# The sums of the exponentials on GpSimd: 512 columns at a time into two sums used in turn, in place of 1024 columns into one double sum

## The reference, cut to what matters

```python
q = (query @ wq.T + bq).reshape(B, SQ, H, HD).transpose(0, 2, 1, 3)
k = (key @ wk.T + bk).reshape(B, -1, H, HD).transpose(0, 2, 1, 3)
v = (value @ wv.T + bv).reshape(B, -1, H, HD).transpose(0, 2, 1, 3)
scores = jnp.einsum('bhqd,bhkd->bhqk', q, k) / jnp.sqrt(jnp.asarray(HD, q.dtype))
attn = jax.nn.softmax(scores, axis=-1)
ctx = jnp.einsum('bhqk,bhkd->bhqd', attn, v)
ctx = ctx.transpose(0, 2, 1, 3).reshape(B, SQ, D)
return ctx @ wo.T + bo
```

## Time and profile before

| | |
|---|---|
| time, median of 3 runs | 1692.62 us (1683.69 to 1693.33) |
| time of the profiled execution | 1690.8 us |
| its span, first to last instruction | 1689.0 us |
| PE busy, share of the span | 1619.8 us, 96% |
| DVE busy | 1179.0 us, 70% |
| ACT busy | 950.8 us, 56% |
| POOL busy | 899.7 us, 53% |

### The profile page before, as it was taken

How to read it: one execution, slowest core, us unless ns; L and a number is a source line. 1 busy time by engine, 2 the same in 40 slices (tenths; PEclk the granted TensorE clock), 3 DMA queues, 4 the chain that set the end, 5 groups by cost and what they waited for, 6 DMA issues and landing times. The chain is left out here.

```text
span 1689.0 us, 36984 instructions
## 1 busy us (share of the span) xinstructions
PE 1619.8 (96%) x15589; PEld 1314.5 (78%) x15604; DVE 1179.0 (70%) x1523; ACT 950.8 (56%) x1437; POOL 899.7 (53%) x472
## 2 busy tenths in 40 slices
PE   7999999999999999999999999667998899999999
PEld 6788888888888888888888887556886677777787
DVE  5137888888888888888888887877434577653322
ACT  4347776777767777777777776662103677630000
POOL 0026788888878878888887885002000344522220
PEclk9999999999999999999999999788999799899999
DMA  5332222222222222222222210213422111211001
GB/s 187 75 50 35 36 39 40 39 38 37 38 37 42 36 36 40 41 36 37 37 40 37 40 24 5 80 53 113 165 88 94 38 51 51 65 50 50 28 23 50
DMA packets 310404, 88.75 MB, mean 53 GB/s; under 512 B 259392, under 2 KB 292160, under 8 KB 310240
## 3 DMA queue, kind: packets, MB, share of 16 engines
q1 hardware_dynamic: 310240, 86.39, 22.2%
HBM read 71.67 MB, written 14.68 MB: 51 GB/s over the span
## 5 line engine op out<-in xcount | busy, mean ns | idle before, releaser
L655 POOL TENSOR_TENSOR b_acc<-b_acc,b_s 128x1024 f32<-128x1024 f32 x168 | 563.6, 3355 | 12.4 <-ACT b_s L854 5.3
L892 DVE TENSOR_TENSOR b_s<-b_s,b_mb 128x2048 f32<-128x2048 f32 x128 | 398.0, 3111 | 28.4 <-ACT b_mb L837 28.4
L929 DVE TENSOR_TENSOR b_mx<-b_psS,b_mx 128x512 f32<-128x512 f32 x480 | 330.8, 689 | 93.3 <-PE b_psS L720 80.2
L854 ACT ACTIVATE b_s<-b_s 128x2048 f32<-128x2048 f32 x128 | 244.3, 1909 | 18.3 <-DVE b_s L892 15.2
L871 ACT ACTIVATE b_s<-b_psS 128x2048 f32<-128x2048 f32 x128 | 241.2, 1885 | 20.9 <-DVE b_mx L929 20.9
L43 PE MATMUL b_work<-wvT,cT 128*128 128x512 f32 x496 | 202.9, 409 | 0.0
L43 PE MATMUL b_work<-cT,wkT 128*128 128x512 f32 x496 | 200.3, 404 | 1.7 <-POOL b_ones L636 1.7
L44 PE MATMUL b_work<-wvT,cT 128*128 128x512 f32 x496 | 194.5, 392 | 0.0
L44 PE MATMUL b_work<-cT,wkT 128*128 128x512 f32 x496 | 194.2, 392 | 0.0
L45 PE MATMUL b_work<-wvT,cT 128*128 128x512 f32 x496 | 193.8, 391 | 0.0
L45 PE MATMUL b_work<-cT,wkT 128*128 128x512 f32 x496 | 193.4, 390 | 0.0
(11 more groups left out here) (290 smaller groups left out, 2802.4 us busy)
## 6 DMA issues: line engine op xcount, KB each, us to landing
cin<-in_ctx SPq DMA_DIRECT2D x480, 64.0 KB, 2.4
experts_sb<-in_L_ffn_expert_w SPq DMA_DIRECT2D x8, 1024.0 KB, 5.3
q_scratch<-d_st SPq DMA_DIRECT2D x16, 256.0 KB, 2.3
k_scratch<-d_st SPq DMA_DIRECT2D x16, 256.0 KB, 2.3
e_q<-q_scratch SPq DMA_DIRECT2D x16, 256.0 KB, 2.7
k_sb<-k_scratch SPq DMA_DIRECT2D x16, 256.0 KB, 2.9
cin<-in_ctx SPq DMA_DIRECT2D x4, 512.0 KB, 8.4
b_kT<-in_x SPq DMA_DIRECT2D x4, 512.0 KB, 8.0
```

What stands on the lines that cost most here:

```text
L655: nc.gpsimd.tensor_tensor(acc[:, :, :], acc[:, :, :], s[:, buf, 2 * i:2 * i + 2, :], ALU.add).then_inc(sum_done, 1)
L854: nc.scalar.activation(part, part, ACT.Exp, scale=SCALE).then_inc(exp_done, 1)
L892: nc.vector.tensor_tensor(s[:, n % BUFS, :, :], s[:, n % BUFS, :, :], mb[:, :].rearrange("p (o n) -> p o n", o=1).broadcast_to([P, CHUNK, ...
L929: nc.vector.tensor_tensor(mx[:, :, :], part, mx[:, :, :], ALU.max).then_inc(mx_done, 1)
```

## The change

The adds work on one block of 512 columns at a time. `b_acc` keeps its size of 128 x 2 x 512, but its two halves are now two sums, and slot m uses half m % 2. The first chunk of a slot makes three adds (block 0 plus block 1, then blocks 2 and 3), each other chunk four: 15 instructions of 512 columns a slot in place of 7 of 1024. Each after the first waits for the one before on `sum_done`. The first add of slot m now waits for `od_full` of slot m - 2 and not of slot m - 1. PE makes the denominators with four products in place of eight. `ADDS`, the number of `sum_done` steps in a slot, and `sums_of`, from which ACT knows when a buffer of `b_s` is free, follow.

```diff
-        ADDS = 2 * CHUNK - 1
+        ADDS = CHUNK * CHUNK - 1
...
                 pool.wait_ge(exp_done, n + 1)
-                if c == 0:
-
-                    if m:
-                        pool.wait_ge(od_full, m)
-                    nc.gpsimd.tensor_tensor(acc[:, :, :], s[:, buf, 0:2, :], s[:, buf, 2:4, :],
-                                            ALU.add).then_inc(sum_done, 1)
-                else:
-                    for i in range(2):
-                        pool.wait_ge(sum_done, m * ADDS + 2 * c - 1 + i)
-                        nc.gpsimd.tensor_tensor(acc[:, :, :], acc[:, :, :], s[:, buf, 2 * i:2 * i + 2, :],
+                for i in range(CHUNK):
+                    if c == 0 and i == 0:
+                        if m >= 2:
+                            pool.wait_ge(od_full, m - 1)
+                    elif c == 0 and i == 1:
+                        nc.gpsimd.tensor_tensor(acc[:, m % 2, :], s[:, buf, 0, :], s[:, buf, 1, :],
+                                                ALU.add).then_inc(sum_done, 1)
+                    else:
+                        pool.wait_ge(sum_done, m * ADDS + 4 * c + i - 1)
+                        nc.gpsimd.tensor_tensor(acc[:, m % 2, :], acc[:, m % 2, :], s[:, buf, i, :],
                                                 ALU.add).then_inc(sum_done, 1)
...
-            return m * ADDS + 2 * c + 1
+            return m * ADDS + 4 * c + 3
...
             def denominators(m):
                 pe.wait_ge(sum_done, (m + 1) * ADDS)
-                for i in range(2):
-                    for j in range(HG):
-                        last = nc.tensor.matmul(psO[j * HD:(j + 1) * HD, P:2 * P], ones[:, :],
-                                                acc[:, i, j * P:(j + 1) * P], start=i == 0, stop=i == 1)
+                for j in range(HG):
+                    last = nc.tensor.matmul(psO[j * HD:(j + 1) * HD, P:2 * P], ones[:, :],
+                                            acc[:, m % 2, j * P:(j + 1) * P], start=True, stop=True)
                 last.then_inc(od_full, 1)
```

## The result

| | before | changed |
|---|---|---|
| time, median | 1688.15 us (1683.69 to 1693.33, 4 runs) | 1709.34 us (1708.12 to 1711.06, 4 runs) |
| ratio | | 1.0125, 95% interval 1.0085 to 1.0166 |
| span of the profiled execution | 1689.0 us | 1707.4 us |

How many runs of a set fall into which group moves its median: two of the four runs before in the table are at 1684, none of the changed ones is at 1700. So I also compare at equal clock, by the medians of each group over all runs: 1709.4 against 1692.6 is +17 us, and 1700.6 against 1684.0 is +16.6 us. The change makes the kernel 1% slower.

What follows compares the result with a forecast made beforehand. PE was taken to bound the kernel before, and POOL, narrowly, the changed one. PE's waiting of 15.1 us less 7.8 saved gave +7.3, so from 1692.6 to 1700 us, range 1683 to 1717.

Steps and rivals of the forecast that it cites:

- That PE paced and the wait of 127.8 us was free: PE set the pace at 32.43 us a slot; POOL's wait until PE has read `b_acc` was worth nothing by itself.
- The adds and the collisions: POOL's slot: adds 20.07 us, low parts 5.04, four collisions with DVE's subtractions at 1.95 each, 7.80; in all 32.91.
- The four products: PE's denominators: eight records fewer save 0.28 us a slot, 7.8 us in all, giving a PE slot of 32.15 us.
- The lead: POOL's last add ends 5.19 us before PE asks; 4.64 left after the change, used up in 6 slots.
- The sum: Whole execution: 15.1 us of PE waiting for POOL less 7.8 us saved on products, +7.3 us.
- a gap of 0.14 us between dependent adds: Rival on POOL's adds: POOL bounds by more than 1.1 us a slot, +24.5 us, time 1717; chance 0.13.
- between "same" and "slower": Outcome classes for the whole time: same, within about 1% (17 us), chance 0.84; slower, beyond that, 0.13.
- That PE keeps the pace: Rival: POOL's slot fits within PE's 32.15 us, so PE paces and the time is 1685 us; chance 0.21.
- That DVE's shorter subtractions pay: Rival on DVE: subtractions wait at most 1.29 us each behind shorter adds; said to give no time, no chance of its own.

Runs made afterwards that it cites:

- both folds: Kernel before plus one add folding the sum's two halves, four products: ratio 0.9938; the same with 14 narrow adds on alternating halves: ratio 0.9942.

## Why the prediction held, and where its terms were off

**That PE paced and the wait of 127.8 us was free.** Right: with that wait put back into the changed kernel, its time stays the same.

**The adds and the collisions.** 20.07 us was predicted for the fifteen adds. The rows of the slot above give 1.37 + 2.62 + 5.34 + 5.36 and 7.26 - 1.9 = 5.36, in all 20.05. The low parts take 5.0 us as predicted. Four collisions a slot came as worked out, but at 3 x 2.05 + 1.9 = 8.0 us, not 7.80: three of the four now hold up a low part, which waits for no predecessor, so there is no dependence gap for the subtraction to hide in. POOL's slot is 33.07 to 33.11 us in place of 32.91.

**The four products.** Mis-sized. Eight records fewer save 0.57 - 0.36 = 0.21 us, not 0.28: some 0.15 us does not go with the number of records. That it is the turn from wide to narrow products is likely, but no run shows it. PE's slot would be 32.22 us, which the first and the last interval of the changed kernel and all those of both folds show, and the whole saving 27 x 0.20 = 5.4 us between the first and the last denominators, not 7.8.

**The lead.** This is the step that failed: 4.64 us of it were said to hide six slots of lag. The kernel before, in its first slot (the low part after the last add, and PE's denominators):

```profile
171.72 1.29 POOL L639 TENSOR_TENSOR cT<-cin,cT 128x512 fp32r<-128x512 f32 x1
```

```profile
177.57 0.64 PE L757 MATMUL b_psO<-b_acc,b_ones 128*32 128x128 f32 x16
```

The changed kernel at the same place and in the two slots after:

```profile
168.45 7.43 POOL L655 TENSOR_TENSOR b_acc<-b_acc,b_s 128x512 f32<-128x512 f32 x4
175.84 3.34 POOL L639 TENSOR_TENSOR cT<-cin,cT 128x512 fp32r<-128x512 f32 x1
...
209.09 3.33 POOL L639 TENSOR_TENSOR cT<-cin,cT 128x512 fp32r<-128x512 f32 x1
...
244.23 1.27 POOL L639 TENSOR_TENSOR cT<-cin,cT 128x512 fp32r<-128x512 f32 x1
```

In the first slot the lead was 177.57 - 171.72 = 5.85 us before and is 178.49 - 175.84 = 2.65 after (the changed kernel's first L756 starts at 178.49; everything in its trace starts 0.92 us later, which takes no part in the lead). It lost 3.2 us at once, the growth of all fifteen adds, where I had taken off only the growth of the last chunk: POOL's rest lies ahead of the first chunk, and from there on its chunks stand back to back, so that each one's growth pushes the next. By the second slot, with L756 at 210.71, the lead is 1.62. The third takes POOL 244.23 - 209.09 = 35.14 us, since it meets five subtractions in this slot (four low parts of 3.3 us and a chunk of 7.31), and it is done 1.3 us after PE would have asked. PE waits from the third slot on, not from the seventh.

**The sum.** From the first to the last denominators the kernel before takes 27 x 32.42 = 875.3 us and the changed one 1071.08 - 178.49 = 892.6, +17.3 us: 892.6 - 27 x 32.22 = 22.7 of waiting (predicted 15.1) less 5.4 saved (predicted 7.8), in place of +7.3. The profile's own list of waits has 20.7, with ends of products that are modelled. Of the 7.6 us more waiting, 26 x 0.12 = 3 us is the larger lag a slot (0.88 against 0.76), 4.64 - 2.65 = 2.0 the mis-sized lead, and 35.14 - 33.11 = 2.0 the fifth collision of the third slot; 0.5 is left over.

So the move was more than twice the forecast one. The time lay inside the range all the same, and partly by luck: the range reached up to 1717 for a gap of 0.14 us between dependent adds, and that gap didn't come (adds start 1.37 us apart, as forecast). By the equal-clock comparison the move is 1.0%, on the line between "same" and "slower".

**The rivals.** That PE keeps the pace is excluded by the 20.7 us of waits. That DVE's shorter subtractions pay: DVE is busy for 64 us less in 143 to 1060, and nothing came of it.

## What to carry to other kernels

An engine at 83% beside one at 100% that sets the pace is not free: before giving it more and shorter instructions, count its whole period, with collisions, against the period of the other. Lead is lost by everything that grew since the engine's last rest, not by the last step alone. Where a sum must get narrower, keep the wide adds and fold once; where adds must be narrow, alternate two sums so that only the fold waits for its neighbour. Both were faster here than the kernel before.

## What the runs showed of the hardware

DVE's 128x2048 subtraction takes 1.9 us from POOL when the instruction that it holds up would have waited for its predecessor anyway: the second add of a pair before (6.76 for 4.84), an add inside a chunk of the changed kernel (7.26 for 5.36). It takes 2.05 us when the one held up waits for nothing: a low part (3.28 to 3.32 for 1.25), or the first add of a chunk, as in the first slot of the changed kernel (175.84 - 168.45 = 7.39 for 5.36). A subtraction of 128x1024 takes 0.9 us. "SBUF — State Buffer" of the Trainium skill, section "Who interferes with whom", gives an exclusive lock held for the whole instruction; the halving with the length of DVE's instruction agrees.

An add of 128x512 that waits for its predecessor starts 1.37 us after it, one that waits for nothing 1.25.

The two traces of the changed kernel, with 0.973 and 0.980 of granted clock on average, are 1707.4 - 1698.9 = 8.5 us apart. Of these, 1.1 lie ahead of the first denominators, none between the first and the last (892.6 and 892.5 us, at a granted clock of 1.00), and 7.3 behind them. Why an execution takes the one or the other, no run here shows.
